# Graph convolutions of three chunks moved between the GRU steps of a two-layer graph network

## The reference

```python
def _graph_conv(x, adj, W, b):
    A = adj + jnp.eye(n); deg = jnp.sum(A, axis=-1); dinv = where(deg == 0, 0, deg ** -0.5)
    norm_adj = dinv[:, :, None] * A * dinv[:, None, :]
    return relu(einsum('bnm,bme->bne', norm_adj, einsum('bnd,de->bne', x, W)) + b)
# part one: GROUPS of 25, 9, 7, 6 and 6 nodes; widths 128 -> 256 -> 128
for g, idx in enumerate(GROUPS):
    h = _graph_conv(x[:, idx], adj[:, idx][:, :, idx], W1[g], b1[g])
    fused = fused.at[:, idx].add(softmax(fusion_w)[g] * _graph_conv(h, adj_g, W2[g], b2[g]))
x = _layernorm(x + fused)
# part two: h = x; five layers with one shared GRU cell
for l in range(5):
    agg = einsum('bij,bid->bjd', (adj != 0), h @ weight[l])
    gi, gh = agg @ w_ih.T + b_ih, h @ w_hh.T + b_hh        # each in three gates r, z, n
    r, z = sigmoid(gi_r + gh_r), sigmoid(gi_z + gh_z)
    h = (1 - z) * tanh(gi_n + r * gh_n) + z * h
x = _layernorm(x + h * mask)
```

## Time and profile before

| what | value |
|---|---|
| median of three runs | 565.27 us (564.62 to 567.2) |
| profiled execution, its own time | 565.27 us |
| its span in the profile | 563.6 us |
| PE busy | 523.9 us, 93% |
| DVE busy | 438.1 us, 78% |
| ACT busy | 380.2 us, 67% |
| POOL busy | 224.6 us, 40% |
| first matmul of window 0 | 104.29 us after the start |
| granted PE clock, whole span | 0.968 of full |

### The profile page before, as it was taken

One profiled execution on the slowest core, in us unless ns is written; L12 is line 12 of the kernel. 1 busy time (PEld: TensorE's weight loads), 2 busy tenths in 40 slices (PEclk: granted clock), 3 DMA queues, 4 the chain that ended last, 5 costly groups with the idle time before them and its releaser, 6 DMA issues.

```text
span 563.6 us, 9740 instructions
## 1 busy us (share of the span) xinstructions
PE 523.9 (93%) x2955; PEld 445.9 (79%) x2955; DVE 438.1 (78%) x980; ACT 380.2 (67%) x703; POOL 224.6 (40%) x278
## 2 busy tenths in 40 slices
PE   5876799999999999999999999999999999999970
PEld 3665698888888888888888888888888888888860
DVE  4425577688788889988888898888888988787784
ACT  3331447566776767778878776887787768777753
POOL 6654451033334332444454324444443243343434
PEclk9786999999999999999999999999999999999995
DMA  4556380000000000000000000000000000000002
GB/s 112 143 126 176 94 223 24 0 1 2 0 1 1 1 1 1 1 20 1 19 20 2 20 0 0 19 0 19 19 0 19 1 0 20 2 18 20 2 19 74
DMA packets 34937, 17.16 MB, mean 30 GB/s; under 512 B 4118, under 2 KB 34811, under 8 KB 34907
## 3 DMA queue, kind: packets, MB, share of 16 engines
q1 hardware_dynamic: 32170, 15.47, 10.2%
q0 software_dynamic: 1280, 0.58, 0.7%
q10 hardware_dynamic: 1456, 0.72, 0.4%
HBM read 12.54 MB, written 4.19 MB: 30 GB/s over the span
## 4 chain that ended last, share of the span: by engine, by line
PE 41%; issue 25%; POOL 16%; SPq 10%; ACT 3%; DVE 3%; POOLq 1%; DMA 0%; ACTq 0%; DVEq 0%
POOL dg L461 10%; PE p L1029 9%; PE p L1031 9%; PE p L1030 9%; PE p L1022 6%; SPq L278 4%; PE p L1016 3%; SPq L284 3%; POOL rs L420 3%; POOL nm L418 2%; SPq L290 1%; PE p L967 1%; PE p L997 1%; DVE fused L746 1%; POOL rs L417 1%
## 5 line engine op out<-in xcount | busy, mean ns | idle before, releaser
L461 POOL TENSOR_TENSOR dg<-hT,ng 128x512 f32<-128x512 f32 x80 | 122.6, 1533 | 281.8 <-ACT ng L620 281.8
L1029 PE MATMUL p<-ghi,wf 128*128 128x512 f32 x240 | 101.2, 422 | 0.0
L1029 PE MATMUL p<-hhi,wh 128*128 128x512 f32 x240 | 100.1, 417 | 0.4 <-ACT hhi L595 0.4
L877 DVE SCALAR_TENSOR_TENSOR cg<-p,biasc,rg 128x512 f32<-128x512 f32 x80 | 60.0, 750 | 46.9 <-ACT rg L608 46.9
L1031 PE MATMUL p<-ghi,wf 128*128 128x512 f32 x240 | 94.6, 394 | 0.0
L1031 PE MATMUL p<-hhi,wh 128*128 128x512 f32 x240 | 94.4, 393 | 0.0
L1030 PE MATMUL p<-hlo,wh 128*128 128x512 f32 x240 | 94.2, 393 | 0.0
L1030 PE MATMUL p<-glo,wf 128*128 128x512 f32 x240 | 93.7, 390 | 0.0
L1022 PEld LDWEIGHTS p<-an,nat 128*128 128x128 f32 x640 | 83.4, 191 | 6.3
L1022 PE MATMUL p<-an,nat 128*128 128x128 f32 (+1 forms) x640 | 84.2, 274 | 0.0
L608 ACT ACTIVATE rg<-p,gb 128x512 f32<-128x512 f32 x80 | 55.1, 689 | 33.8 <-PE p L1031 26.8
(11 more groups left out here) (124 smaller groups left out, 809.5 us busy)
## 6 DMA issues: line engine op xcount, KB each, us to landing
xn<-in_x_dram SPq DMA_DIRECT2D x8, 512.0 KB, 5.1
an<-in_adj_dram SPq DMA_DIRECT2D x8, 512.0 KB, 7.4
out_dram<-tile_data SPq DMA_DIRECT2D x16, 256.0 KB, 2.3
w<-in_L_gnn_W_dram SPq DMA_DIRECT2D x2, 640.0 KB, 4.9
tile_data<-in_x_dram SPq DMA_DIRECT2D x16, 50.0 KB
tile_data<-in_x_dram POOLq DMA_DIRECT2D x16, 24.0 KB, 2.5
zg<-in_L_gnn_weight_dram ACTq DMA_DIRECT2D x1, 320.0 KB, 4.2
tile_data<-in_x_dram SPq DMA_DIRECT2D x8, 36.0 KB
```

What stands on the lines that cost most here:

```text
L461: nc.gpsimd.tensor_tensor(dg[:, w.slot % 2, :], hT[:, w.slot, :], ng[:, w.slot % 2, :], ALU.subtract).then_inc(d_ok, 1)
L877: STT(cg[:, p, :], PH[:], bhn, rg[:, p, :], ALU.add, ALU.mult).then_inc(t1_ok, 1)
L1029: MM(bank[:], w[:, 0, cols], xhi, start=start, stop=False)
```

## The change

Only chunk 0's graph convolution stays in the prologue. Those of chunks 1 to 3 are cut into nine pieces, and piece by piece they are placed in windows 2 to 10 of the preceding chunk's 20 windows (`Plan`). On PE a piece stands after the z product with the state and before `turn`. On ACT and DVE a piece stands at the end of the engine's program of its window. The degrees and the spreading of a chunk after next go into windows 12, 14 and 15. Since the steps now need six PSUM banks, a piece has two (`PL`, `PM`), one of them shared with slots that enter, and the aggregation has one bank (`PG`) instead of two; this brings waits that weren't there (`if c:`). `back` packs four graphs into a transpose, 4 transposes instead of 16. The prologue aggregates only slots 0 and 1; slots 2 and 3 enter in windows 0 and 1. The second layer norm works in place in `xn` and is spread over windows 2 to 15. All loops on registers are gone: every engine's program is written out.

```diff
+class Plan:
+    ONES = 0
+    ADJ, Y, HA, HB, SA, SB, OUT, GATHER, BACK = 2, 3, 4, 5, 6, 7, 8, 9, 10
+    DEGREES, SCALED, SPREAD = 12, 14, 15
+    STATS1 = {11 + 2 * j + h: (j, h) for j in range(SLOTS) for h in range(2)}
+    APPLY1 = {(13 + 2 * j + h) % PER: (j, h) for j in range(SLOTS) for h in range(2)}
+    STATS2 = {2 + 4 * j + h: (j, h) for j in range(SLOTS) for h in range(2)}
+    APPLY2 = {4 + 4 * j + h: (j, h) for j in range(SLOTS) for h in range(2)}
...
-        PR, PH, PZ, PI, PT, PX = P[:6]
-        PG = P[6:8]
+        PR, PH, PZ, PI, PT, PG, PL, PM = P
+        SHARED = dict(adj=(PL, PM), y=(PL, PM), ha=(PL, PM), hb=(PL, PM), s=(PL, PM, PL), o=(PM, PL), f=PL)
...
+            for visit in range(SLOTS):                          # POOL, before the steps
+                deviation1(visit)
...
+            norm1(0)                                            # ACT, before the steps
+            norm1(1)
+            begin(0, PL)
+            aggregated(0)
+            norm1(2)
+            begin(1, PM)
+            aggregated(1)
+            norm1(3)
...
+                if w.turn == "step":                            # ACT, end of a window
+                    act.wait_ge(h_ok, k)
+                    nc.scalar.copy(hhi[:, w.prev, :], hT[:, w.prev, :]).then_inc(hi_ok, 1)
+                if c is not None:
+                    if w.i == Plan.ADJ:
+                        adjacency(c)
...
+                    if w.i == Plan.OUT:
+                        output(c)
...
+                if w.turn == "step":                            # DVE, end of a window
+                    lo_state(k + 3)
+                if c is not None:
+                    if w.i == Plan.ONES:
+                        ones(c)
...
+                    if w.i == Plan.GATHER:
+                        gather(c)
+                    if w.i == Plan.BACK:
+                        add(c)
+                if w.sg + 2 < CHUNKS and w.i == Plan.DEGREES:
+                    degrees(w.sg + 2)
...
+            norm2(final - 3)                                    # DVE, behind the steps
+            leave(final - 1, PT)
+            norm2(final - 2)
+            end_step(WINDOWS, SLOTS - 1)
...
             def back(c):                                        # PE
                 pe.wait_ge(gathered, ADDS * (c + 1))
-                for q in range(4):
-                    for i in range(4):
+                for t in range(CB // PACK):
...
+                product(PZ, wh, 1, xhi, xlo, True, False)       # PE, in each window
+                c = next_chunk(w)
+                if c is not None:
+                    if w.i == Plan.ADJ:
+                        pe.wait_ge(hi_ok, k + 2)
+                        adjacency(c)
+                    if w.i == Plan.Y:
+                        neighbours(c)
...
+                    if w.i == Plan.BACK:
+                        back(c)
+                if w.out:
+                    pe.wait_ge(h_ok, k - 1)
+                    turn(PT, lambda q: hT[:, w.old, q * 128:(q + 1) * 128])
...
+                if w.feed:
+                    pe.wait_ge(glo_ok, k + 2)
+                    pe.wait_ge(nat_ok, w.turned + 1)
+                    aggregate(k + 2, lambda q: nat[:, w.old, q, :])
```

More of the change, by code:

```diff
@@ L31 @@
 FN = 25
+NP = 32
+PACK = 128 // NP
 HID = 256
@@ L68, in runs, with visit_of, layer_of @@
     return [tuple(r) for r in out]
+def visit_of(k):
+    return (k // PER) * SLOTS + k % SLOTS
+def layer_of(k):
+    return (k % PER) // SLOTS
 class Window:
[L83 to L93, removed]
@@ L96, in opening @@
[L96 to L136, removed]
@@ L139, in windows, with __init__ @@
[L139 to L145, removed]
-        yield opening(sg + 1)
-    yield from supergroup(eng, CHUNKS - 1, more=False, unrolled=unrolled)
-    yield None
+    def __init__(self, k):
+        self.k, self.sg, self.i, self.l, self.slot = k, k // PER, k % PER, layer_of(k), k % SLOTS
+        self.prev, self.old = (k - 1) % SLOTS, (k - 2) % SLOTS
+        self.turn = None if k < 1 else "step" if layer_of(k - 1) < LAYERS - 1 else "leave"
+        self.out = None if k < 2 else "step" if layer_of(k - 2) < LAYERS - 1 else "leave"
+        coming = visit_of(k + 2) if k + 2 < WINDOWS else B // SB
+        self.enter = coming if layer_of(k + 2) == 0 and coming < B // SB else None
+        self.feed = self.out == "step" or self.enter is not None
+        self.left = visit_of(k - 2) if self.out == "leave" else None
+        self.turned = None if self.out != "step" else (k - 2) // PER * (PER - SLOTS) + (k - 2) % PER
@@ L471, in _ @@
+            for visit in range((CHUNKS - 1) * SLOTS, B // SB):
+                deviation2(visit)
         @block.scalar
@@ L488, in _, with adjacency, neighbours @@
                 nc.scalar.copy(wf[:, l, 0, :], P[WF_BANKS[l]][:, 0:GATES]).then_inc(prep_hi, 1)
+            def adjacency(c):
+                act.wait_ge(t_ps, 2 * c + 1)
+                bank = banks(c)["adj"][0]
+                for t in TA:
+                    r, o = ROWS[t], OFF[t]
+                    last = nc.scalar.activation(na[0:r, o:o + r], bank[0:r, o:o + r], ACT.Identity, scale=dinv[0:r, c, t:t + 1])
+                last.then_inc(na_ok, 1)
+            def neighbours(c):
+                act.wait_ge(y_ps, 2 * c + 1)
+                nc.scalar.copy(ya[:], banks(c)["y"][0][:, 0:COLS_A]).then_inc(ya_ok, 1)
@@ L630, in _ @@
+            for visit in range((CHUNKS - 1) * SLOTS, B // SB):
+                norm2(visit)
         @block.vector
@@ L810, in _, with lo_state @@
-            with dve.Fori(0, CHUNKS - 2) as c:
-                chunk(c, True)
-            chunk(CHUNKS - 2, False)
-            for s in range(SLOTS):
-                settle(s, s * SB, s + 1)
-            gather(CHUNKS - 1)
-            def lo_state(m, s):
+            add(0)
+            for visit in range(SLOTS):
+                norm1(visit)
+            def lo_state(m):
                 dve.wait_ge(hi_ok, m + 1)
-                TT(hlo[:, s, :], hT[:, s, :], hhi[:, s, :], ALU.subtract).then_inc(lo_ok, 1)
@@ L989, in output, with back @@
                     last.then_inc(o_ps, 1)
[L991 removed]
+            def back(c):
                 pe.wait_ge(gathered, ADDS * (c + 1))
[L994 to L1002 removed]
@@ L1003, in _ @@
[L1003 to L1011 removed]
+                for t in range(CB // PACK):
+                    last = TR(banks(c)["f"][:, t * D:(t + 1) * D], fused[:, t * 128:(t + 1) * 128], ident[:])
+                last.then_inc(f_ps, 1)
+            pe.wait_ge(prep_lo, 1)
```

852 lines of the change are left out of this document (396 added, 456 removed).

## The result

The changed kernel took 616.81 us, the median of 4 runs (613.28 to 617.29), against 564.94 for the kernel before (563.07 to 567.20, 4 runs): ratio 1.090, 95% interval 1.085 to 1.096. It is slower; 610 was forecast. The profiled execution took 616.46 us with a span of 614.2, 50.6 more than the span before. One run of the kernel with three edits, further down, took 1053.92 us where its five others took 560.34 to 561.65; its ratio is made without that run, and no trace shows what happened in it.

The account below looks back on a forecast made before the run. PE's own work was taken to bound the loop, an engine-to-engine chain the prologue. Terms -52.0 + 39.3 + 2.5 + 41.5 + 6.5 + 5.0 + 1.7 = +44.5 on 565.27 gave 610 us (599 to 621).

Parts of the forecast that it names:

- prologue: Ahead of window 0: with one chunk, window 0 starts at 52.3 us (46 to 58) instead of 104.3, 52.0 less.
- PE's added work: Step loop on PE: 13.1 us a chunk of graph convolution, 39.3 for three (36 to 41), paid in full.
- two entries, windows 0 and 1: PE in windows 0 and 1: each entering slot adds an aggregation (0.8) and a transpose (about 0.45), 2.5 us.
- direct waits at the pieces: PE waits at pieces for the ends of ACT's and DVE's programs: 41.5 us over three chunks (10 to 52).
- DVE beyond its room: DVE pieces (`add`, degrees, adjacency flags) exceeding its idle time in a window delay the state: 6.5 us (3 to 12).
- clock: Behind the wait at BACK, PE runs 3.3 us at half clock, half lost, three times: 5.0 us (0 to 10).
- tail: Behind the steps: the second norm of two visits now comes there, 1.7 us more (0 to 3).
- BACK: Window 10, transposes of the convolution's output: PE waits 4.3 us for `gather`, in each chunk.
- Y: Window 3: PE waits for half B's scaling on DVE, 1.2 us, or 1.85 with norm work.
- rival A: Loop: one piece's wait lets ACT and DVE get ahead, direct waits and DVE excess vanish; 558 us, chance 0.05.
- rival B: Loop: inputs come about 1 us earlier, 21 waits lose some 20 us; 590 us, chance 0.15.
- rival C: Loop: clock falls at five more waits of 1.2 us or longer per chunk, 15 x 1.65 = 25 us; 635 us, chance 0.11.

Follow-up runs that it names:

- kernel with three edits: Changed kernel with all PE pieces behind the aggregation at their window's end, 64 bytes per partition behind `fused`, POOL's spread in window 17 instead of 15: 560.85 us.
- the traces with the gaps: Changed kernel with an unused 64, 128 or 192 bytes per partition of SBUF placed behind `fused`: 616.49, 615.17 and 614.84 us.
- the two tries at DVE: To the kernel with three edits, degrees in window 8 instead of 12, or `add` split over windows 10 and 11: 560.66 and 560.93 us.
- a kernel whose PE was otherwise full: The kernel with three edits, with only BACK put back ahead of the transpose of the old state in window 10: 572.14 us.

## Why the prediction was right, and where it was off

The direction, the main mechanism (PE waits at the pieces for the ends of other engines' programs) and the size of the total were right; the size is in part luck, as the last point shows. By its own steps, with the measured number in us (windows as above):

| term | predicted | measured |
|---|---|---|
| prologue | -52.0 | -55.3 |
| PE's added work | +39.3 | +37.0 |
| two entries, windows 0 and 1 | +2.5 | +2.7 |
| direct waits at the pieces | +41.5 | +33.6 |
| DVE beyond its room (with POOL's queue) | +6.5 | +11.0 |
| clock | +5.0 | +18 |
| matmul pitch (address) | 0 | +4.0 |
| tail | +1.7 | -0.4 |
| sum | +44.5 | +50.6 |

- *Prologue and PE's work.* Both from rows of the same operations, both within 3.3 us. Window 0 came at 48.99 in the range 46 to 58.
- *Waits.* BACK was 4.3 a piece, measured 3.9; `yb` 6.1 in all against 5.4, `hb` 5.85 against 6.1, the three copies of OUT 7.4 against 6.4. Too high were Y (4.9 against 3.1: PE waits 1.0 to 1.1 in each chunk, and for ACT's `na` ahead of half A, not for DVE's half B as forecast), HB (2.25 against 0.9), and the aggregation behind OUT (2.1 against 0.2: ACT had room). The choice for the full sum, since a wait carries the others' programs along, was right; rival A is out with 39.4 us idle, and rival B with 33.6 of 41.5 left.
- *DVE and POOL.* The 11.0 is what the other rows leave of the loop's 106.3, and so no measurement of its own. PE's listed waits for gates, transpose and aggregation make up 5.6 of it. 2.1 of these is the wait in window 38, for which the prediction, with "POOL's `power` and `spread` lie in its idle time", had nothing. That step failed: idle time over the loop is not room at the place. The row of pitch is the other term that it had at nothing ("windows without a piece still 5.46 us"): 0.05 in 79 windows, measured in plain ones.
- *Clock.* This is the term that was mis-sized. The forecast charged one stretch for each BACK, and there it was nearly right: four parts, some 6.1 us (half of the time at the lower level that isn't wait), against 5.0. It put the shorter waits at nothing, and behind seven of nine of them the clock fell too, some 12 us. Its ground was that the only fall among its rows stood behind 3.4 us without a matmul. The trace of before had two more falls in the prologue, which these rows leave out: one begins within a wait of 1.81 us, one 0.9 us behind a wait of 2.50 (two waits of PE, then the stretches at 0.50, columns as in rows 1):

```profile
19.30 2.00 PE L948 MATMUL p<-na,tile_data 100*128 100x100 f32 x8 [1.81 <-DMA tile_data<-in_x_dram]
...
38.24 1.26 PE L948 MATMUL p<-na,tile_data 100*128 100x100 f32 x8 [2.50 <-DMA tile_data<-in_x_dram]
```

```profile
18.60:25.40 6.80, 6.10 (x22) 5.14 (x23) 1.19 (x4) 1.60 (x5) 4.39 (x7) 0.50 0.57 124
39.10:52.70 13.60, 9.15 (x35) 7.29 (x34) 5.52 (x21) 3.05 (x8) 3.05 (x4) 0.50 0.58 148
```

So a fall behind a wait of about 2 us could have been priced before the result. The measured case is rival C in its mechanism, with eleven parts where C counted eighteen, and the measured time lies between the forecast and C. C's fifteen was itself too many: the forecast's own list has four more waits of 1.2 us or longer in each chunk, not five, and that makes twelve. The Trainium skill says in "TensorE: Matmul & The Clock Gate", section HAM oscillation, that waits between bursts can put the clock back for each burst; the changed kernel agrees (0.97 in the loop, ten falls behind twelve waits), while of all the waits of 1.9 to 2.3 us in these traces 26 of 53 agree, and of the three of 3.15 us one.
- *Cancelling errors.* The waits were 7.9 too high, the prologue's gain 3.3 too small, PE's work 2.3 and the tail 2.1 too high; clock, pitch and DVE were 21.5 too low. The total is nearer than its terms, and that is luck. The clock's 18 isn't: though single waits differ, the traces with the gaps, which have the same twelve waits, show ten, eleven and ten parts.

What the change could have been worth follows from the measured column: -55.3 + 37.0 + 2.7 = -15.6 us with no wait, no fall and the old addresses. With the three repairs the span is 5.0 shorter than before (558.6 against 563.6). The other 10.6 lie in windows 11 to 14 and 18 of each chunk (2.6, 4.2 and 4.1 us together over the kernel before). There norm and graph work share DVE, ACT and POOL; the two tries at DVE changed single windows and hardly the sum, so which of them holds it isn't shown.

## What to carry to other kernels

Before a piece of work goes into a full engine's program, compare two times in the window: when that engine reaches the place, and when the other engines' programs, at whose ends the inputs are made, are over. Moving the same instructions 3 us later in the window was worth 50.7 us of 616.8 here. For the clock, count 1.6 us on top of every second wait of about 2 us on TensorE (26 of 53 here; in single traces from three to seven of nine), and up to 3 on top of one of 3.9, at which the clock fell each time here, mostly for a double stretch. And look at each engine's queue at the place itself, even if it is only a third busy.

## What was not expected of the hardware

- TensorE's plain window of 18 products of 512 columns, 4 transposes and 8 small products took 5.475, 5.480, 5.513 or 5.529 us, with nothing changed but the SBUF address of its operands, in steps of 64 bytes. The value 5.513 was seen in one trace. All of the tensors behind `fused` moved together, so which of them it is stays open.
- The granted clock fell at all 15 waits of 3.8 to 4.0 us, at 26 of 53 of 1.9 to 2.3 us, and at one of three of 3.15 us in a kernel whose PE was otherwise full. In the changed kernel alone it was ten of twelve. A single stretch cost 1.6 us.
